# A fused pooling and feed-forward kernel: h moved in two halves, residual and bias adds placed later, two tiles' splits moved, z rescaled two banks at a time

## The reference

```
attn_in = tanh(x @ W1 + b1);  scores = attn_in @ v
p = softmax(where(mask, scores, -1e30));  pooled = (p @ x) / cnt
r = pooled                                   # the residual of the layer
h = (r - mean) * rsqrt(var + 1e-5) * gamma + beta
y = silu(h @ dequant(fc1) + fc1_bias)        # 512 -> 2048
z = y @ dequant(fc2) + fc2_bias              # 2048 -> 512
out = x + r + 0.5 * z
```

## Time and profile before

| | us |
|---|---|
| median of 3 runs (1325.63 to 1328.93) | 1327.86 |
| the profiled execution, its own time | 1327.16 |
| its span, first to last instruction | 1325.4 |
| PE busy / DVE / ACT / POOL | 1290.2 / 1069.8 / 1009.2 / 201.5 |
| one batch in the middle (643.33 to 722.61) | 79.28 |

### The profile page before, as it was taken

The page is one execution under the profiler, slowest core; times in us unless marked ns, Lnnn a source line. Parts: engine busy times, 40 slices in busy tenths (PEclk is TensorE's granted clock), DMA queues, the critical chain, the costliest instruction groups (busy, mean ns, idle before and its releaser), DMA issues.

```text
span 1325.4 us, 20199 instructions
## 1 busy us (share of the span) xinstructions
PE 1290.2 (97%) x5851; PEld 992.9 (75%) x5851; DVE 1069.8 (81%) x2063; ACT 1009.2 (76%) x1661; POOL 201.5 (15%) x166
## 2 busy tenths in 40 slices
PE   7888999999999999999999999999999999999998
PEld 5665877777777777777777777777777777777787
DVE  6999888888788788888888788888878888888744
ACT  3676777877787887778877788877787877778775
POOL 3302111030301203011030301203021020301100
PEclk7999999999999999999999999999999999999999
DMA  7962103131140322213131230313213031230100
GB/s 226 229 217 32 65 15 66 49 64 65 29 101 1 64 65 49 81 17 66 47 64 66 35 94 1 65 66 57 72 19 80 32 64 65 38 90 1 33 32 32
DMA packets 274235, 84.54 MB, mean 64 GB/s; under 512 B 250026, under 2 KB 250692, under 8 KB 273604
## 3 DMA queue, kind: packets, MB, share of 16 engines
q1 hardware_dynamic: 272944, 82.96, 26.4%
q10 hardware_dynamic: 1172, 0.08, 0.1%
HBM read 51.47 MB, written 16.86 MB: 52 GB/s over the span
## 4 chain that ended last, share of the span: by engine, by line
PE 73%; DVE 13%; ACT 6%; issue 4%; SPq 2%; DMA 1%; ACTq 0%; DVEq 0%
PE y_ps L1182 14%; PE z_ps L1210 14%; PE y_ps L1183 13%; PE z_ps L1213 13%; PE z_ps L1212 8%; SPq L442 2%; DVE scratch L919 2%; ACT y_ps L658 2%; ACT L603 1%; DVE z_ps L972 1%; PE a_ps L1141 1%; PE a_ps L1092 1%; DVE y_lo L963 1%; PE a_ps L1093 1%; PE a_ps L1094 1%
## 5 line engine op out<-in xcount | busy, mean ns | idle before, releaser
L658 ACT ACTIVATE y_ps<-y_ps,ratio 128x512 f32<-128x512 f32 x768 | 474.1, 657 | 153.9 <-PE y_ps L1183 152.1
L1210 PE MATMUL z_ps<-w_hi,y_hi 128*128 128x512 f32 x1024 | 414.0, 404 | 11.4 <-DVE z_ps L972 7.4
L1182 PE MATMUL y_ps<-hT_hi,w 128*128 128x512 f32 x1016 | 409.2, 403 | 7.7 <-ACT y_ps L658 5.3
L1213 PE MATMUL z_ps<-w_hi,y_lo 128*128 128x512 f32 x1024 | 400.8, 391 | 0.0
L1183 PE MATMUL y_ps<-hT_lo,w 128*128 128x512 f32 x1016 | 397.5, 391 | 0.0
L963 DVE TENSOR_TENSOR y_lo<-y_f,y_hi 128x512 fp32r<-128x512 f32 x256 | 198.8, 777 | 146.1 <-ACT y_hi L571 144.9
L1210 PEld LDWEIGHTS z_ps<-w_hi,y_hi 128*128 128x128 f32 x1024 | 192.7, 188 | 84.9 <-issue 25.6
L1182 PEld LDWEIGHTS y_ps<-hT_hi,w 128*128 128x128 f32 x1016 | 191.1, 188 | 86.3 <-ACT y_ps L658 33.4
L1212 PE MATMUL z_ps<-w_lo,y_hi 128*128 128x512 f32 x640 | 249.8, 390 | 0.0
L652 ACT ACTIVATE y_f<-y_ps,vec_cols,mant 128x512 f32<-128x512 f32 x256 | 185.1, 775 | 73.8 <-PE y_ps L1183 73.4
L493 POOL TENSOR_TENSOR x<-x,scratch 128x512 f32<-128x512 f32 x64 | 91.6, 1434 | 941.6 <-ACT scratch L632 941.6
(11 more groups left out here) (207 smaller groups left out, 1166.3 us busy)
## 6 DMA issues: line engine op xcount, KB each, us to landing
x<-in_x_dram SPq DMA_DIRECT2D x64, 256.0 KB, 3.2
out_dram<-x SPq DMA_DIRECT2D x64, 256.0 KB, 2.7
x_cols<-in_x_dram SPq DMA_DIRECT2D x240, 64.0 KB, 2.2
h_cols<-scratch SPq DMA_DIRECT2D x224, 64.0 KB, 2.1
fc_codes<-in_L_ffn_fc_q_dram SPq DMA_DIRECT2D x8, 1024.0 KB, 12.5
fc_scaled<-units_dram SPq DMA_DIRECT2D x4, 1024.0 KB, 17.8
e<-powers_dram SPq DMA_DIRECT2D x3, 1024.0 KB, 15.6
h_rows<-powers_dram SPq DMA_DIRECT2D x1, 1024.0 KB, 10.8
```

The source lines that it names most:

```text
L658: nc.scalar.activation(y_ps[k % 2][:], y_ps[k % 2][:], ACT.Copy, scale=ratio[:, c * NF + k:c * NF + k + 1]).then_inc(scaled, 1)
L1182: mm(o, w, hT_hi[:, c, :], start=(c == 0), stop=False, skip_group_check=True)
L1210: mm(z_ps[r][:], y_hi[k % 2][:, rows], w2_hi[:, k, :], start=(k == 0), stop=False, skip_group_check=True)
L1213: last = mm(z_ps[r][:], y_lo[k % 2][:, rows], w2_hi[:, k, :], start=False, stop=(k == NF - 1 or k in WHOLE), skip_group_check=True)
```

## The change

- `normalise` writes into another buffer (`e1[0]`, free after the weights are made), laid out as two halves of columns, and no longer waits for the residual adds (but for the first sequence). `move_h` moves each half with 16 transfers of 32 x 8 pieces, 32 transfers in all, with a semaphore for each half. `TURNH` 0 and 1 stay in slot 24 and wait for the first half; `TURNH` 2 goes behind `SPLITH` 0 in slot 25 and waits for the second, `TURNH` 3 behind `SPLITH` 1 in slot 26.
- POOL's residual adds wait until all four blocks are normalised, its bias adds until the last `SPLITH` is done. DVE's `TURN` 0 waits for the residual adds, since they read `scratch`.
- `y_hi` of tile 5 is made by DVE in slot 9 (`cast_y`) in place of ACT in slot 8. `y_lo` of tile 9 is made ahead of `normalise` (in the last batch in slot 16).
- The four `z_ps` banks are one tensor `z_all`, and `rescale_z` multiplies two banks in one instruction, once both blocks are complete.

```diff
-        z_ps = [bank(f"z_ps{r}") for r in range(NJ)]
+        z_all = ctx.enter_context(nc.psum_tensor("z_all", [P, NJ, 512], F32))
+        z_ps = [z_all[:, r, :] for r in range(NJ)]
...
-        DVE_MOVED = {24: [("TURNH", 0), ("TURNH", 1), ("TURNH", 2), ("TURNH", 3)], 25: [("SPLITH", 0)], 26: [("SPLITH", 1)],
+        DVE_MOVED = {24: [("TURNH", 0), ("TURNH", 1)], 25: [("SPLITH", 0), ("TURNH", 2)], 26: [("SPLITH", 1), ("TURNH", 3)],
...
+        Y_CAST = 5
+        Y_SOON = 9
+        Y_AT = 16
...
+        normal = e1[0][:].rearrange("p j d -> p (j d)").rearrange("p (h j d) -> p h j d", h=2, j=NJ)
...
                 sp.wait_ge(h_ready, a * NJ + NJ)
-                for i in range(P // Q):
-                    for j in range(P // Q):
-                        piece = slice(j * Q, (j + 1) * Q)
-                        sp.dma_start(h_cols[piece, :, i * Q:(i + 1) * Q], rows[i * Q:(i + 1) * Q, :, piece]).then_inc(h_moved, 16)
+                for half in range(2):
+                    blocks = slice(half * 2 * NJ, (half + 1) * 2 * NJ)
+                    rows = normal[:, half, :, :].rearrange("p j (c d) -> p (j c) d", d=P)
+                    for i in range(P // Q):
+                        for j in range(P // Q):
+                            piece = slice(j * Q, (j + 1) * Q)
+                            sp.dma_start(h_cols[piece, blocks, i * Q:(i + 1) * Q],
+                                         rows[i * Q:(i + 1) * Q, :, piece]).then_inc(h_moved[half], 16)
...
-                pool.wait_ge(pooled_done, a * NJ + (J + 1))
+                if is_first(a):
+                    pool.wait_ge(pooled_done, J + 1)
+                elif J == 0:
+                    pool.wait_ge(h_ready, a * NJ + NJ)
...
-                elif J == 0:
-                    pool.wait_ge(h_ready, a * NJ + NJ)
+                if J == 0:
+                    pool.wait_ge(hT_done, a * ND + ND)
...
-                    if i % 4 == 0:
+                    if i % 4 == 0 and i // 2 + 1 != Y_CAST:
                         y_hi_part(b, i // 2 + 1)
...
+                if s == 0:
+                    dve.wait_ge(res_added, a * NJ)
...
-                if r < NJ - 1:
-                    dve.wait_ge(z_part, z_part_count(b, k, r))
+                if r + 1 < NJ - 1:
+                    dve.wait_ge(z_part, z_part_count(b, k, r + 1))
...
-                v.tensor_tensor(z_ps[r][:], z_ps[r][:], z_ratios[WHOLE.index(k)], ALU.mult).then_inc(z_scaled, 1)
+                two = z_all[:, r:r + 2, :]
+                row = z_ratios[WHOLE.index(k)].rearrange("p (o d) -> p o d", o=1).to_broadcast([P, 2, D])
+                v.tensor_tensor(two, two, row, ALU.mult).then_inc(z_scaled, 1)
...
+                        if name == "H" and not is_first(b):
+                            split_y(b, Y_SOON)
```

More of the change, by code:

```diff
@@ L203, in build @@
         turned = sem("turned")
-        h_moved = sem("h_moved")
+        h_moved = [sem(f"h_moved{half}") for half in range(2)]
         h_turned = sem("h_turned")
@@ L316, in z_count @@
         def z_count(b, k, r):
-            return b * NZ + WHOLE.index(k) * NJ + r + 1
+            return b * NZ // 2 + WHOLE.index(k) * NJ // 2 + r // 2 + 1
         def z_part_count(b, k, r):
@@ L344, in xt_buffers, with by_halves @@
             return first_xt(s) if is_first(a) else (xt_rows[s], hi[:], lo[:])
+        normal = e1[0][:].rearrange("p j d -> p (j d)").rearrange("p (h j d) -> p h j d", h=2, j=NJ)
+        def by_halves(ap):
+            return ap.rearrange("p (h d) -> p h d", h=2)
         def w1_views(k0):
@@ L436, in move_h @@
             def move_h(a):
-                rows = scratch[:, 0:NJ * D].rearrange("p (n d) -> p n d", d=P)
                 sp.wait_ge(h_ready, a * NJ + NJ)
-                for i in range(P // Q):
-                    for j in range(P // Q):
-                        piece = slice(j * Q, (j + 1) * Q)
-                        sp.dma_start(h_cols[piece, :, i * Q:(i + 1) * Q], rows[i * Q:(i + 1) * Q, :, piece]).then_inc(h_moved, 16)
+                for half in range(2):
[6 more added lines that the diff above has]
+                                         rows[i * Q:(i + 1) * Q, :, piece]).then_inc(h_moved[half], 16)
             def turn(b, p):
@@ L496, in bias @@
                 pool.wait_ge(res_added, a * NJ + (J + 1))
-                if J == 0 and is_first(a):
-                    pool.wait_ge(hT_done, ND)
-                elif J == 0:
-                    pool.wait_ge(h_ready, a * NJ + NJ)
+                if J == 0:
+                    pool.wait_ge(hT_done, a * ND + ND)
                 nc.gpsimd.tensor_tensor(xt[p][:, J, :], xt[p][:, J, :], b2h[:], ALU.add).then_inc(bias_added, 1)
@@ L801, in turn_columns @@
             def turn_columns(a, s, p, ch):
-                if s == 0 and by_pe(a - 1):
-                    dve.wait_ge(h_tr, a * ND)
+                if s == 0:
+                    dve.wait_ge(res_added, a * NJ)
+                    if by_pe(a - 1):
+                        dve.wait_ge(h_tr, a * ND)
                 dve.wait_ge(cols_in[s], a * 64)
@@ L917, in normalise @@
                 for J in range(NJ):
-                    dve.wait_ge(res_added, a * NJ + (J + 1))
-                    v.tensor_scalar(pooled[J], pooled[J], mv[:, J, 0:1], rstd[1][:, J:J + 1], ALU.subtract,
+                    if is_first(a):
+                        dve.wait_ge(res_added, J + 1)
+                    o, i = (pooled[J], pooled[J]) if is_first(a) else (normal[:, :, J, :], by_halves(pooled[J]))
+                    v.tensor_scalar(o, i, mv[:, J, 0:1], rstd[1][:, J:J + 1], ALU.subtract,
                                     ALU.mult).then_inc(h_ready, 1)
             def turn_h(a, c, p, ch):
-                if c == 0:
-                    dve.wait_ge(h_moved, (a - 1) * 256)
-                chunk = h_cols[:].rearrange("p (j c) n -> p j c n", j=NJ)[:, :, c, :]
+                if c % 2 == 0:
+                    dve.wait_ge(h_moved[c // 2], (a - 1) * 256)
+                chunk = h_cols[:].rearrange("p (h j c) n -> p h j c n", h=2, j=NJ)[:, c // 2, :, c % 2, :]
                 v.transpose(by_block(h_rows[:, c, :]), chunk).then_inc(h_turned, 1)
@@ L963, in split_y, with cast_y @@
                 v.tensor_tensor(y_lo[k % 2][:], y_f[k % 2][:], f32(y_hi[k % 2][:]), ALU.subtract).then_inc(split_done, 1)
+            def cast_y(b, k):
+                dve.wait_ge(silu_done, b * NF + k + 1)
+                dve.wait_ge(fc2_done, b * NF + (k - 1))
+                v.tensor_copy(y_hi[k % 2][:], y_f[k % 2][:]).then_inc(yhi_done, 1)
             def rescale_z(b, k, r):
-                if r < NJ - 1:
-                    dve.wait_ge(z_part, z_part_count(b, k, r))
+                if r + 1 < NJ - 1:
+                    dve.wait_ge(z_part, z_part_count(b, k, r + 1))
                 else:
@@ L986, in ffn @@
                         split_y(b, (i + 1) // 2)
-                    if i % 4 == 1:
+                    if i % 4 == 1 and (i // 2 + 1 != Y_SOON or is_first(b)):
+                        if i // 2 + 1 == Y_CAST:
+                            cast_y(b, Y_CAST)
                         split_y(b, i // 2 + 1)
                     if (i - 1) // 2 in WHOLE:
-                        for r in (2 * ((i - 1) % 2), 2 * ((i - 1) % 2) + 1):
-                            rescale_z(b, (i - 1) // 2, r)
+                        rescale_z(b, (i - 1) // 2, 2 * ((i - 1) % 2))
                     if i == SLOTS - 1:
@@ L997, in ffn @@
                     for ahead, name, n in cond_steps(b, i, DVE_PLAN_FIRST if is_first(b) else DVE_PLAN, DVE_TURN, DVE_MOVED):
+                        if name == "H" and not is_first(b):
+                            split_y(b, Y_SOON)
                         steps[name](b + ahead, n, p if ahead == 2 else 1 - p, chains[ahead])
+                    if is_last(b) and i == Y_AT:
+                        split_y(b, Y_SOON)
                     if is_first(b):
@@ L1160, in transpose_h @@
                 for J in range(NJ):
-                    last = nc.tensor.transpose(a_ps[c % 2][:, J * P:(J + 1) * P], pooled[J][:, c * P:(c + 1) * P], ident[:])
+                    last = nc.tensor.transpose(a_ps[c % 2][:, J * P:(J + 1) * P], normal[:, c // 2, J, (c % 2) * P:(c % 2 + 1) * P], ident[:])
                 last.then_inc(h_tr, 1)
```

## The result

| | us | against before |
|---|---|---|
| before, median of 4 runs (1325.63 to 1328.93) | 1328.16 | |
| changed, median of 4 runs (1431.29 to 1435.09) | 1434.16 | 1.0798, 95% interval 1.0777 to 1.0819 |
| forecast | 1351.0, range 1312 to 1405 | |

What follows compares the result with a forecast made beforehand. PE, busy 97% of the span, was taken as the bound, so only its stalls could move. Per batch -0.4 - 0.25 + 0 + 0.4 + 1.9 = +1.65, times 14 = +23.1, gave 1351 us, range 1312 to 1405.

Steps and rivals of the forecast that it cites:

- the cost of a half move: SP's move of h: 0.49 us per half transfer, 0.53 with the step, so DVE waits for the second half: +1.9 a batch.
- the rival: "Twice as long": half moves cost SP 0.62 to 0.70 us each, DVE and PE stand: about 1424 us, chance 0.24.
- the clock: In the rival "twice as long", PE standing so long drops to 1.2 GHz, costing some 1 us more a batch.
- Bias adds: End of a batch: POOL's bias adds collide with DVE's y_lo of tile 15 and part_lo: +0.4, ends 0 and +1.6.
- z two banks: DVE's multiply of 1024 columns takes about 1.2 us; gains and later bank release cancel: 0, bounds -0.1 and +0.3.
- y_lo of tile 9: Made ahead of normalise, it closes PE's gap at fc2 of tile 9: -0.4 us a batch; the move starts 0.6 later.
- y_hi of tile 5: Moved from ACT to DVE, it lets the late silu start earlier, then wait for PE's fc1 step: -0.25 us a batch.
- its end with all gaps on ACT closed: Lowest end of the case that the halves fit, with no collision cost either: 1312 us.
- The bias eats it: Rival: the half moves fit, but the bias-add collisions cost 0.7 to 1.2 a batch: 1324 to 1333 us, chance 0.11.
- the likeliest case: The forecast case, a half move at 0.49 to 0.60 us: 1351 us, own range 1333 to 1370, chance 0.34.
- The sign: Whole kernel: slower by more than about 0.3% (4 us) with chance 0.57, faster 0.31, within 0.12.
- the halves fit: Rival: a half move costs at most 0.48 us with its step, DVE's wait is gone: 1317 to 1323 us, chance 0.31.

Runs made afterwards that it cites:

- the fourth: The kernel before with only the two splits moved, y_hi of tile 5 to DVE and y_lo of tile 9 ahead of normalise: 1331.3 us, 1.0021 of before.
- the sixth run: The kernel before with only y_lo of tile 9 made ahead of normalise, y_hi of tile 5 staying on ACT: 1334.3 us, 1.0055 of before.
- the first run: The changed kernel with h moved in 16 whole transfers and one semaphore, as before the change: 1353.8 us, 1.0199 of before.

## Why the prediction was wrong

- **The step that failed: the cost of a half move.** The bounds were right (0.35 and 0.70 with what lies between), the value was taken in the middle, "the rest halved", from a single comparison of two forms that differed in source and in the layout of the destination as well. Measured: 0.611, and 0.677 with the step, 32 in 21.65 us. The row for the upper end stood there, 1408 pieces for 0.69 us against 64 for 0.59: 0.1 us for 1344 more pieces, which for the 256 pieces of a half gives 0.02, just the measured difference of 0.629 and 0.611. It was outweighed by an argument about form that no row carried. What the prediction took for the other queue from DMA: Bandwidth & Descriptors in the Trainium skill, section "Anatomy of one DMA — SWDGE (gpsimd) path", that many descriptors can be emitted before their cost shows, gave the right end too; the trace agrees, 0.611 against 0.629. With 0.677 in the forecast's own sum the second half lands 32 x (0.677 - 0.53) = 4.7 us later, which makes 1351 + 14 x 4.7 = 1417: this one term, without the clock, is 66 of the 83 us by which the forecast was off.
- **What followed from it** went as the rival said: second half landing at 22.9 us after the move's start (rival 23.9), DVE standing 6.3 us. The rival's parts were sized wrongly in both directions: PE late by 4.8 on average and not 6.3, the clock 2.2 and not 1.0. That its sum, 7.3, is near the 7.0 measured is luck in part. Undone alone the halves give back 5.7 a batch, since PE then waits for `part_lo`.
- **Bias adds: forecast +0.4 with an upper end of 1.6, measured 1.5** beside whole moves; behind the halves most of it is hidden, as the 2.7 us of waiting for `part_lo` show. The collision was found, with its place. The size assumed that ACT's wait would take up part and that one instruction would be hit; both were hit, one after the other, 0.7 and 1.1 us.
- **z two banks: forecast 0 within -0.1 and +0.3, measured +0.2 (beside whole moves) and +0.4 (beside halves), neither clear of the noise.** The duration, 1.22, was as estimated. The waits at tiles 4 and 10 (0.5 and 0.8 us) are larger than I thought, but other gaps shrink for them, and at tile 10 a gap of 0.4 us stays with one bank at a time.
- **y_lo of tile 9: forecast -0.4, measured +0.5** (1334.3 against 1326.8, by 14). The gap went as forecast. What I did not work through is that everything behind `normalise` moves by 0.6 us: the bias adds onto tile 10's `y_lo`, and h, whose path I had myself called just in time.
- **y_hi of tile 5: forecast -0.25, measured -0.28 in the traces** (3.0 us of the run's time, 0.2 a batch, by the fourth against the sixth run). Mechanism and size were right: the silu starts earlier and then waits for PE's own `fc1` step, as the forecast said. What it does not touch is the larger gap behind the exponentials, which runs from 648.40 and ends with a scaling ahead of `y_hi` at 650.07; the forecast had put both down to the same cause, and its end with all gaps on ACT closed did not come.
- **Two ranges of the forecast don't follow from its terms.** "The bias eats it" is -0.75 with +0.7 to +1.2, which makes 1327 to 1334 and not 1324 to 1333. And the likeliest case's own range, 1333 to 1370 for 0.49 to 0.60, starts below what 0.49 gives (1351) and ends far below what 0.60 gives (3.5 us a batch later, 1400).
- **The sign was right, but the chance of it was not well founded.** Had the halves fitted, the kernel would still have been near the 1354 us of the first run, 2% slower; "the halves fit" at 1317 to 1323 had 0.31.

Left open: at the end of every second batch, where PE's loop starts again, the changed kernel shows a wait that ends with nothing the profile names, up to 1.4 us against 0.4 before (5.3 us in all against 1.3). And how much of the two banks' cost is real, which is near what these runs can tell.

## What to carry to other kernels

Here a move's cost on the queue that issues it belonged to the transfer, not to its pieces: before you split a move to get its first part sooner, multiply the whole issue time by the number of parts and see when the last one lands. Where a path is just in time, price a delay at every consumer behind it, since a gap that you close at one place opens at the next late thing; only when the collision and the landing were mended along with it did the split become part of a gain. And put GpSimd's work beside the instructions of VectorE that read PSUM, not wherever GpSimd happens to be free.

## What the runs showed of the hardware

- SP's time for a transfer from SBUF to SBUF over 32 rows: 0.629, 0.611, 0.601 us for 16, 8, 4 pieces of 128 bytes on a row; 0.49 with as many pieces from DRAM, laid side by side, back to back; 0.35 for `x_cols`.
- Each of 14 stalls of 4.1 to 5.1 us brought PE's granted clock to 0.50, in two of them only after PE had started again; the 12 steps behind a stall took 4.3 to 5.3 us in place of 2.7.
- A two-operand VectorE subtraction of 0.69 us took 1.36 to 1.80 us beside GpSimd adds; multiplies with one operand in PSUM are not touched, one by one (0.62) or as 128 x 1024 (1.22).
